# Layer 0's end reordered: gate-up products between the last output products, half 0's routing among the attention units

## What is computed

```python
x = x + L0_xattn(layernorm(x), ctx, ctx, ...)        # 32 heads of 16, 8 key heads
h = layernorm(x)
scores = sigmoid(h @ gate_w.T) + bias                # 16 experts
topk_w, topk_idx = top_k(scores, 4)
topk_w = topk_w / sum(topk_w)
out = sum over the 4 chosen experts of topk_w * ((silu(h @ Wg) * (h @ Wu)) @ Wd)
out = out + (silu(h @ Sg.T) * (h @ Su.T)) @ Sd.T     # shared expert, every row
x = x + out
```

## Time and profile before

| | us |
|---|---|
| median of 3 runs | 1272.04 (1270.81 to 1272.21) |
| the profiled execution | 1268.94 |
| its span in the profile | 1267.5 |
| TensorE busy with matmuls | 1205.7 (95%) |
| VectorE busy | 819.0 (65%) |
| ScalarE busy | 682.0 (54%) |
| GpSimd busy | 387.3 (31%) |

### The profile page before, as it was taken

The page is one execution under the profiler, slowest core; times in us unless marked ns, Lnnn a source line. Parts: engine busy times, 40 slices in busy tenths (PEclk is TensorE's granted clock), DMA queues, the critical chain, the costliest instruction groups (busy, mean ns, idle before and its releaser), DMA issues.

```text
span 1267.5 us, 16304 instructions
## 1 busy us (share of the span) xinstructions
PE 1205.7 (95%) x5820; PEld 930.8 (73%) x5820; DVE 819.0 (65%) x1529; ACT 682.0 (54%) x1561; POOL 387.3 (31%) x446
## 2 busy tenths in 40 slices
PE   8699987999999999899999999998999999999997
PEld 5556545767667677688888888877888888888765
DVE  4457765777776776665566666774455666667757
ACT  2245563167777787344555555662445555556621
POOL 3400010457777775002232322230022323222200
PEclk9899998999999999999999999999999999999999
DMA  8645240297579856521121221120311212211101
GB/s 292 149 122 140 52 180 38 100 336 171 103 155 242 254 116 129 183 83 41 44 67 59 67 59 42 59 83 25 92 38 47 67 59 64 62 42 51 58 1 66
DMA packets 73327, 127.91 MB, mean 101 GB/s; under 512 B 12120, under 2 KB 31448, under 8 KB 70552
## 3 DMA queue, kind: packets, MB, share of 16 engines
q1 hardware_dynamic: 54592, 76.00, 19.6%
q0 software_dynamic: 17296, 48.26, 15.1%
q10 hardware_dynamic: 1360, 2.62, 0.5%
HBM read 150.37 MB, written 26.48 MB: 140 GB/s over the span
## 4 chain that ended last, share of the span: by engine, by line
PE 68%; DVE 10%; issue 7%; POOL 7%; DMA 4%; ACT 3%; SPq 1%; ACTq 0%; POOLq 0%; DVEq 0%
PE bank L458 52%; PE bank L1935 7%; PE bank L1911 4%; POOL moe L1510 4%; POOL xs L1499 2%; PE bank L667 2%; DVE rden L853 1%; POOL wf_raw L1489 1%; DMA wf_raw<-in_wffn,weight_row 1%; PE bank L639 1%; PE bank L654 1%; PE bank L434 1%; DMA q0st<-m0T 1%; DMA q_rows<-q0T_lo 1%; DVE stats L395 1%
## 5 line engine op out<-in xcount | busy, mean ns | idle before, releaser
L1903 POOL TENSOR_SCALAR p<-p,mx 128x256 f32<-128x256 f32 x256 | 163.2, 653 | 521.8 <-DVE mx L1897 521.8
L1095 DVE TENSOR_TENSOR wf_lo<-wf_raw,wf_hi 128x512 fp32r<-128x512 f32 x192 | 124.4, 689 | 33.9 <-ACT wf_hi L1089 29.3
L1889 ACT ACTIVATE p<-bank,mx 128x256 f32<-128x256 f32 x256 | 118.0, 485 | 10.7 <-DVE mx L1879 10.6
L458 PE MATMUL bank<-xnA_hi,w1q_hi 128*128 128x512 f32 x288 | 118.5, 411 | 3.6 <-DVE xnA_lo L452 3.2
L1089 ACT ACTIVATE wf_hi<-wf_raw 128x512 fp32r<-128x512 f32 x192 | 110.2, 626 | 8.5 <-DMA wf_raw<-in_wffn,weight_row 8.1
L458 PE MATMUL bank<-xnA_hi,w1q_lo 128*128 128x512 f32 x288 | 114.6, 398 | 0.0
L458 PE MATMUL bank<-xnA_lo,w1q_hi 128*128 128x512 f32 x288 | 114.0, 396 | 0.0
L1918 ACT ACTIVATE p1T_hi<-bank 128x512 fp32r<-128x512 f32 x128 | 75.2, 596 | 65.7 <-PE bank L1911 65.7
L1843 ACT ACTIVATE q1T_hi<-bank 128x512 fp32r<-128x512 f32 x64 | 38.2, 597 | 132.5 <-PE bank L458 132.4
L458 PE MATMUL bank<-w1o_hi,a1T_hi 128*128 128x512 f32 x256 | 105.2, 411 | 0.1
L458 PE MATMUL bank<-wf_raw,zT 128*128 128x512 f32 x220 | 102.9, 593 | 2.2 <-DVE x L1169 1.3
(11 more groups left out here) (327 smaller groups left out, 3006.6 us busy)
## 6 DMA issues: line engine op xcount, KB each, us to landing
w_raw<-in_wq SPq DMA_DIRECT2D x64, 256.0 KB
w_raw<-in_wo SPq DMA_DIRECT2D x64, 256.0 KB
moe<-xn SPq DMA_DIRECT2D x2, 2304.0 KB, 10.4
returned<-moe SPq DMA_DIRECT2D x8, 512.0 KB, 7.7
q0st<-q_rows SPq DMA_DIRECT2D x14, 256.0 KB, 4.2
x<-in_x SPq DMA_DIRECT2D x8, 256.0 KB, 5.6
ctx<-in_ctxT SPq DMA_DIRECT2D x2, 1024.0 KB, 10.1
k0bd<-k_rows SPq DMA_DIRECT2D x16, 128.0 KB, 2.4
```

Source lines behind the costliest of these rows:

```text
L458: ins = nc.tensor.matmul(ps, a, b, start=(n == 0), stop=(n == len(pairs) - 1))
L1095: nc.vector.tensor_tensor(wf[m % 2][1][:, a, c, :], raw[m % STREAMS][:, a, c, :], wf[m % 2][0][:, a, c, :].bitcast(F32), ALU.subtract).the ...
L1889: ins = nc.scalar.activation(pr1[s % 2][:, h, :], banks.of(("s1", s, n))[:, hh * 2 * P:(hh + 1) * 2 * P], ACT.Exp, bias=m[:, UH + h:UH + h ...
L1903: ins = nc.gpsimd.tensor_scalar(pr1[s % 2][:, h, :], pr1[s % 2][:, h, :], m[:, 3 * UH + h:3 * UH + h + 1], 1.0, ALU.mult, ALU.mult)
```

## The change

The loop over the units ends at step 63. Group 2's norm goes to steps 39 to 53, the gate's weights to 46, the gate product of half 0 to 54, its sigmoid to 55, its transposes to 58, the choice of experts of half 0 to 59, and the ranks of half 0 to 61 (`tensor_ranks_first`); gate-up 0 stands at 56 behind output product 5. Behind the loop come output product 6, gate-up 1, output product 7. ScalarE makes a square root of no use to anyone there, before the last halves of a0T, which loads the table. `vector_slots_first` makes half 0's rows of the table, and `row_hot` is made in two halves, the first into a tile of its own. `tensor_shared`, `scalar_shared` and `vector_shared` have a new order, with every bank named; the table of tokens stands behind gate-up 6 instead of gate-up 7. Seven constants of GpSimd are made before the wait for the last unit instead of behind it. The diff, cut to its core:

```diff
-        EXPERTS_FROM = UNITS0 // 2 + 4
         LAG_Y = 9
+        SPLIT_AT = {38: 0, 40: 1, 42: 2, 44: 3}
+        NORM2_AT = {39: 0, 43: 1, 45: 2, 47: 3, 49: 4, 51: 5, 53: 6}
+        GATE_SPLIT, GATE_AT, GATE_TURN_AT, CHOICE_AT, RANKS_AT = 46, 54, 58, 59, 61
...
-            for i in range(-LEAD_S, UNITS0 + LAG_Y + 1):
+            for i in range(-LEAD_S, UNITS0):
                 if i + LEAD_S < UNITS0:
                     scores(i + LEAD_S)
                 if 0 <= i + LEAD_T < UNITS0:
                     turned_scores(i + LEAD_T)
                 opening_steps(i, lambda k: norm_turn(1, k, next(fill)), lambda v: values(v, next(fill)),
-                              lambda: keys(1, next(fill)), lambda m: query(1, m, next(yrs)), lambda: maxima(0))
+                              lambda: keys(1, next(fill)), lambda m: query(1, m, 7), lambda: maxima(0))
                 if 0 <= i < UNITS0:
                     attend(i)
                 b = of_batch(i, LEAD_S)
                 if b:
                     maxima(b)
-                before_experts(i, nothing, nothing,
-                               lambda j: norm_turn(2, j - 3, next(yrs)) if j >= 3 else None,
-                               lambda: tensor_gate(0, next(yrs)))
+                if NORM2_AT.get(i, 0) >= 3:
+                    norm_turn(2, NORM2_AT[i] - 3, 7 if i < UNITS0 - LEAD_S else next(srs))
+                if i == GATE_AT:
+                    tensor_gate(0, 0)
                 b = of_batch(i, 1 - LAG_Y)
                 if b is not None:
-                    project_out(b)
-            tensor_gate_turn(0, next(yrs))
+                    project_out(b, 7)
+                if i == GATE_AT + 2:
+                    tensor_gate_up(0, 6)
+                if i == GATE_TURN_AT:
+                    tensor_gate_turn(0, 1)
+                if i == RANKS_AT:
+                    tensor_ranks_first(0)
+            project_out(B - 2, 7)
+            tensor_gate_up(1, 2)
+            project_out(B - 1, 3)
...
-                if i >= HB and i % HB == 0 and i <= UNITS0:
+                if i >= HB and i % HB == 0:
                     sums_out((i - 1) // KV0, (i // HB - 1) % 2)
-                if i == EXPERTS_FROM:
+                if i in SPLIT_AT:
                     act.wait_ge(S["q0_mm"], 2 * KT)
                     act.wait_ge(S["k0_mm"], 2)
                     act.wait_ge(S["v0_mm"], B)
-                before_experts(i, scalar_expert_weight, scalar_gate_weights,
-                               lambda j: norm(2, j), lambda: scalar_gate(0))
+                    scalar_gu(0, SPLIT_AT[i])
+                if i == GATE_SPLIT:
+                    scalar_gate_weights()
+                if i in NORM2_AT:
+                    norm(2, NORM2_AT[i])
+                if i == GATE_AT + 1:
+                    scalar_gate(0)
                 b = of_batch(i, -4)
                 if b is not None:
                     attended(b)
+            sums_out(B - 1, 1)
+            nc.scalar.activation(first_col[:, 0:1], eps, ACT.Sqrt)
+            attended(B - 1)
...
-                    if b == B - 2:
-                        for k in range(HB - 1):
-                            dve.wait_ge(S["y0_add"], HB + k + 1)
-                            norm_stats(3, k)
-                before_experts(i, vector_expert_weight, vector_gate_weights,
-                               lambda j: norm(2, j), nothing)
-            vector_gate(0)
+                    if b >= HB:
+                        dve.wait_ge(S["y0_add"], b + 1)
+                        norm_stats(3, b - HB)
+                if i in SPLIT_AT:
+                    vector_gu(0, SPLIT_AT[i])
+                if i == GATE_SPLIT:
+                    vector_gate_weights()
+                if i in NORM2_AT:
+                    norm(2, NORM2_AT[i])
+                if i == CHOICE_AT:
+                    vector_gate(0)
+                    vector_choice(0)
+            vector_slots_first()
+            for h in range(2):
+                reciprocal(B - 1, h)
+                softmax_norm(B - 1, h)
+            attended(B - 1)
+            for b in range(B - 2, B):
+                project_out(b)
+                dve.wait_ge(S["y0_add"], b + 1)
+                norm_stats(3, b - HB)
...
+            if h == 0:
+                dve.wait_ge(S["t0_mm"], KV0 * 6)
...
-        def tensor_ranks():
-
-            ps = banks.take(next(turn_ring), "ranks", (S["at_row"], 1))
+        def tensor_ranks_first(n):
+
+            ps = banks.take(n, "ranks0", (S["row_hot"], 1))
+            pe.wait_ge(S["taken"], 1)
+            pe.wait_ge(S["rank_consts"], 3)
+            flat = taken[:, :, :].rearrange("p b e -> p (b e)")
+            nc.tensor.matmul(ps[:, 0:HB * E0], below[:, :], flat[:, 0:HB * E0], start=True, stop=False)
+            for d in range(1, HB):
+                ins = nc.tensor.matmul(ps[:, d * E0:HB * E0], ones_r[:, :], flat[:, 0:(HB - d) * E0], start=False,
+                                       stop=(d == HB - 1))
+            ins.then_inc(S["ranks"], 1)
+
+        def tensor_ranks(n):
+
+            ps = banks.take(n, "ranks", (S["at_row"], 1))
             pe.wait_ge(S["taken"], 2)
-            pe.wait_ge(S["rank_consts"], RANK_CONSTS)
             flat = taken[:, :, :].rearrange("p b e -> p (b e)")
-            nc.tensor.matmul(ps[:, 0:B * E0], below[:, :], flat, start=True, stop=False)
-            for d in range(1, B):
-                nc.tensor.matmul(ps[:, d * E0:B * E0], ones_r[:, :], flat[:, 0:(B - d) * E0], start=False,
-                                 stop=(d == B - 1))
-            for b in range(B):
-                ins = nc.tensor.matmul(ps[:, B * E0:(B + 1) * E0], ones_r[:, :], taken[:, b, :], start=(b == 0),
-                                       stop=(b == B - 1))
-            ins.then_inc(S["ranks"], 1)
+            for d in range(1, B + 1):
+                first = max(HB, d)
+                nc.tensor.matmul(ps[:, (first - HB) * E0:(HB + 1) * E0], ones_r[:, :],
+                                 flat[:, (first - d) * E0:(B + 1 - d) * E0], start=(d == 1), stop=False)
+            nc.tensor.matmul(ps[:, 0:HB * E0], below[:, :], flat[:, HB * E0:B * E0], start=False,
+                             stop=True).then_inc(S["ranks"], 1)
...
+        def vector_slots_first():
+
+            hs = slice(0, HB)
+            dve.wait_ge(S["ranks"], 1)
+            dve.wait_ge(S["rank_consts"], RANK_CONSTS - 2)
+            vstep.step(nc.vector.tensor_copy(rank0[:, :, :], banks.of("ranks0")[:, 0:HB * E0].rearrange(
+                "p (b e) -> p b e", b=HB)))
+            vstep.step(nc.vector.tensor_tensor(ohr[:, :, :, :], oh[:, hs, :, :],
+                                               rank0[:, :, :].unsqueeze(2).broadcast_to([P, HB, TOP0, E0]), ALU.mult))
+            vstep.step(nc.vector.tensor_reduce(slot_f[:, hs, :], ohr[:, :, :, :], AX.X, ALU.add))
+            vstep.step(nc.vector.tensor_scalar(shifted[:, hs, :], slot_f[:, hs, :], 1.0 / P, -(P - 1.0) / (2 * P),
+                                               ALU.mult, ALU.add))
+            vstep.step(nc.vector.tensor_scalar(shifted[:, hs, :], shifted[:, hs, :], ROUND, None, ALU.add))
+            vstep.step(nc.vector.tensor_scalar(in_tile[:, hs, :], shifted[:, hs, :], ROUND, None, ALU.subtract))
+            vstep.step(nc.vector.scalar_tensor_tensor(out=at_row[:, hs, :], in0=in_tile[:, hs, :], scalar=-float(P),
+                                                      in1=slot_f[:, hs, :], op0=ALU.mult, op1=ALU.add))
...
+        def vector_row_hot(h):
+            if h:
+                dve.wait_ge(S["at_row"], 1)
+            else:
+                dve.wait_ge(S["st_k"], 64)
+            n = PAIRS // 2
+            nc.vector.tensor_tensor(row_hot[h][:, :, :],
+                                    flat(at_row)[:, h * n:(h + 1) * n].unsqueeze(2).broadcast_to([P, n, P]),
+                                    rows_of[:, :].unsqueeze(1).broadcast_to([P, n, P]),
                                     ALU.is_equal).then_inc(S["row_hot"], 1)
...
-            tensor_gate_up(0)
-            for k in range(HB):
-                norm_turn(3, k, next(turn_ring))
-            tensor_gate_up(1)
-            tensor_gate(1, next(turn_ring))
-            tensor_z_turn(0)
-            tensor_z_turn(1)
-            tensor_gate_turn(1, next(turn_ring))
-            tensor_gate_up(2)
-            tensor_ranks()
-            tensor_gate_up(3)
-            for n in (0, 2, 4):
-                if n == 4:
-                    tensor_tokens()
-                tensor_down(n)
-                tensor_down(n + 1)
-                tensor_z_turn(n + 2)
-                tensor_z_turn(n + 3)
-                if n < 4:
-                    tensor_gate_up(n + 4)
-                    tensor_gate_up(n + 5)
-            tensor_down(6)
-            tensor_down(7)
+            tensor_gate_up(2, 4)
+            for k, n in enumerate((1, 7, 5, 3)):
+                norm_turn(3, k, n)
+            tensor_gate_up(3, 1)
```

(66 more changed lines are left out.)

93 lines of the change are left out of this document (39 added, 54 removed).

## The result

| | before | changed |
|---|---|---|
| median of 11 runs each, us | 1270.81 | 1273.51 (1272.05 to 1275.31) |
| ratio, 95% interval | | 1.002 (1.0011 to 1.003) |
| profiled execution, its span, us | 1268.94, 1267.5 | 1273.85, 1272.4 |
| TensorE busy, us | 1205.7 | 1212.9 (95%) |
| VectorE, ScalarE, GpSimd busy, us | 819.0, 682.0, 387.3 | 820.2, 683.7, 385.1 |

The change makes the kernel 2.7 us slower. The forecast was -0.2 us.

What follows compares the result with a forecast made beforehand. TensorE was taken as the bound, reordering giving at most 20 us. An 8 us gain on TensorE was lost to the token-table wait and half clock: first expert product -0.2 us, total 1272.0, own range 1269 to 1275, overall 1264 to 1277.

Steps and rivals of the forecast that it cites:

- S: Start of the last scores product (unit 63's) in the loop: 161.40 us before, forecast 167.3, 5.9 us late.
- T: Time when attend 56 is done in the loop: 172.5 us before, forecast 184.8, 12.3 later.
- A: Rival: the loop absorbs the early norm, ScalarE not held at step 43; up to 7.7 us earlier, 1264.3 us; chance 0.24.
- D: Rival: a ScalarE table switch costs more than its load, at most 1.47 us hidden; 1273.5 us; chance 0.02.
- Rival C: The 3.7 us rest near 153 us halves the clock inside the loop, costing 2.7 to 5 us; chance 0.26.
- From T to the ranks: TensorE's products and waits behind attend 56: ranks done at 224.2 us, 1.5 early, without the half clock at 200 us.
- R: Time when the last ranks are done: 225.7 us before, forecast 224.2.
- the table's gain: Early square-root table load ahead of the last norm: takes 1.28 us off that norm.
- E: Start of the second gate product: 219.6 us before, forecast 218.3.
- From R to the table: Chain on VectorE and GpSimd ends at R + 19.6; TensorE waits 7 us and starts the token table at 243.8.
- From the table to the first expert product: Table 3.5, products 12.4 and half clock 2.3 us: first expert product at 262.0 against 262.21.
- the price of one such fall: Half clock behind the table wait: 2.7 us for 2.8 us of work, taken as 2.3, bounds 0 and 3.5.

Runs made afterwards that it cites:

- e12: Changed kernel without the early square root, with the wait for all eight output products (`y0_mm`) back before the last norm's square root: 1274.02 us, one run.
- e6: Changed kernel with only the early square root, which loads the table, taken out: 1273.33 us.
- e4_warm: Changed kernel plus two products of twelve matmuls that nobody reads, on TensorE ahead of the token table: 1268.97 us, 0.9994 of the kernel before.
- e1_fill: Changed kernel with z 4 and 5, down 4 and 5 and gate-up 7 ahead of the token table on TensorE: 1270.08 us, 1.0002 of the kernel before.
- e3_both: Changed kernel with the edits of e1_fill and e2 together: 1269.48 us, 0.9986 of the kernel before.
- e8_mended: Changed kernel with a new order behind gate-up 6 on TensorE, VectorE and ScalarE to match: 1270.87 us, 0.9993 of the kernel before.
- e9: Changed kernel with e8_mended's order and group 2's norm later, mostly at steps 47 to 53: 1268.43 us, 0.9967 of the kernel before.
- e10: e9 plus nine matmuls that nobody reads on TensorE right before the token table: 1265.27 us, 0.9957 of the kernel before.
- e7_loop_warm: Changed kernel plus one product of twelve matmuls that nobody reads, at step 46 before turned scores 48: 1273.9 us.
- e2: Changed kernel with group 2's norm at steps 39, 47 and 49 to 53 instead of 39 to 53 in twos: 1271.32 us, 1.0001 of the kernel before.

## Why the prediction was wrong

- **The loop, S and T: right.** Exp 46 waits behind the square root, TensorE stands still 3.68 us, the transpose waits 2.06 us for the addition to x, and T came out at 184.8 as forecast (turned scores 56 were 0.2 us later, and the gate product waited 0.99 us instead of 1.6). Rivals A (the loop absorbs the norm) and D (a switch costs more than its load) did not happen: exp's load begins 0.02 us behind the square root and exp starts 1.29 us after it. The Trainium skill (ScalarE: Activation LUTs, What ACT_TABLE_LOAD costs) has a switch at some 2.66 us with its drain; the rows here show 1.28 and no drain.
- **Rival C, half right.** The clock did fall at 158, to 0.51 on average until 165, but S stayed where the forecast without that fall had it. The kernel is slower by the 2.7 us at which C began, but from a fall at another place; that the figures meet is chance.
- **From T to the ranks: right** (R 224.7 against 224.2, and no half clock at the last output product), with one reason wrong: the table's gain came from the dropped wait (e12 against e6, 1.3 us). The terms named between E and R add up to 223.1 and not 224.2; z turns 0 and 1 and the gate turn are not named, and took 1.2 us (220.24 to 221.43).
- **From R to the table: right.** 7 us of waiting were forecast, 6.69 came. R came 0.5 us late and the chain behind it was 0.8 short (tile_hot at R + 18.8 instead of R + 19.6). The reading of the multiplications holds: the first ended 2.6 us after row_hot did (242.05 and 239.43), and the second took 2.76 alone. The Trainium skill (SBUF — State Buffer, Who interferes with whom) says that a VectorE instruction with two inputs in SBUF contends with a GpSimd instruction that reads SBUF. The trace agrees: a multiplication takes 2.6 to 2.8 us and as much more as row_hot runs beside it.
- **From the table to the first expert product: wrong, and this is the miss.** The step took "the price of one such fall" from one product, 5.47 - 2.80 = 2.7, cut it to 2.3, and set 3.5 as its upper bound. Measured: 5.6 (21.98 - 16.41). 2.7 was what one product lost in a fall that lasted 6.8 us (from 199.6 to 206.4; the earlier trace rows shows its start), and that product was all the work TensorE had in it. This one lasted 13.7 us, 12.2 of them behind the table's start. From the table's start to down 4 it took 8.01 us where e4_warm took 4.50, from down 4 to gate-up 7 5.18 instead of 3.14: 3.5 + 2.0, and nothing behind that. The bound should have been all the work between the wait and the first expert product at half rate. ScalarE, which was to hide a part in the down products, hid little: at full clock down 4 waits 0.26 us for it (e4_warm).
- With 5.6 in place of 2.3 the sum is +3.1 us for the stretch; the traces give +3.3 and the medians +2.7. The products of this step at full clock were 0.5 us longer than forecast (16.41 against 15.9) and the table started 0.2 earlier, which is the small rest.

## What to carry to other kernels

A rest that a reordering opens costs its own length and then the half rate of whatever follows, for as long as the clock stays down: price it by the work that falls into the slow stretch behind the rest, not by one instruction group seen once. When work is moved forward on the bounding engine, look at what it needs in all other queues too. Moving TensorE's products alone gave 3.4 us against the changed kernel (e1_fill) and 4.0 with the late norm (e3_both), and both made new waits with the clock down again. The order in which every queue follows gave no more by its median (2.6, e8_mended), though its first expert product came 1.1 us earlier; with the late norm it gave 5.1 (e9), and with the last 2.4 us filled 8 (e10). And where a wait for output product 7 stood before the last norm's square root, the table load came behind all the waits; without it the load went ahead on its own.

## What the runs showed of the hardware

- Behind the rest of 6.7 us the granted clock was at its lower level for 13.6 to 13.7 us in all six traces that have it, 9.7 to 12.2 of them with TensorE at work. Behind the rest of 3.68 us in the loop, and the one of 2.89 us in the kernel before, it was back after 6.8 us.
- Shorter rests went both ways. Behind 2.36 us the clock fell in both traces that have it (e8, e9), 1.0 and 1.6 us after the rest had ended; behind 1.26 and 0.31 us before the table it did not (e4, e10), but at the end of one of 1.40 us it did (e1_fill). 2.50 us brought it down in e3_both and 2.49 didn't in e1_fill; 2.06 us did in e7_loop_warm and didn't in the changed kernel; in the same loop it fell in rests of 2.93 to 2.96 us (e2, e3, e10) and not in or behind one of 2.96 us in e9, where it fell 9 us later. What decides between them the runs don't show.
- The fall of the clock near 39 us lasts 6.8 us in the trace before and 10.2 us in the thirteen others. Whether that is chance or comes with the change one trace before can't tell. Output product 3 moves by up to 2 us among the thirteen.
- ScalarE's load of the square root's table, 1.28 us, ended 4 us ahead of the square root in e6_no_early_table; with the wait for `y0_mm` in front (e12_wait_y0, and the kernel before) it came 0.1 us behind the moments.
